# Extra pieces of seven attention steps moved to the groups without values, projections in pieces of 512 columns

## The reference

```python
xn = layernorm(x)
# attention: 16 heads of 8 channels
q, k, v = heads(xn @ Wq.T), heads(xn @ Wk.T), heads(xn @ Wv.T)
q = q * cos + rotate_half_interleaved(q) * sin     # k alike
attn = softmax(q @ k.T * 8 ** -0.5) @ v
# mixture of 8 experts, the two best of each row
gates = softmax(xn @ gate_w + gate_b); top 2 of 8
h = gelu(xn @ w1[e] + b1[e]); h = gelu(h @ w2[e] + b2[e])
ffn = sum over the two of gate * (h @ w3[e] + b3[e])
out = x + attn + ffn
```

## Time and profile before

| what | us |
|---|---|
| median of 3 runs | 631.75 |
| span of the profiled execution | 630.1 |
| PE busy | 597.7 (95%) |
| ACT busy | 536.9 (85%) |
| DVE busy | 338.4 (54%) |
| POOL busy | 195.7 (31%) |
| steps 2 to 8, from the first exponential of step 2 to the last of step 8 | 86.84 to 299.84 |

### The profile page before, as it was taken

How to read it: one execution, slowest core, us unless ns; L and a number is a source line. 1 busy time by engine, 2 the same in 40 slices (tenths; PEclk the granted TensorE clock), 3 DMA queues, 4 the chain that set the end, 5 groups by cost and what they waited for, 6 DMA issues and landing times.

```text
span 630.1 us, 12248 instructions
## 1 busy us (share of the span) xinstructions
PE 597.7 (95%) x4152; PEld 259.9 (41%) x4152; DVE 338.4 (54%) x819; ACT 536.9 (85%) x548; POOL 195.7 (31%) x187
## 2 busy tenths in 40 slices
PE   9889999999999999998999999999999999999996
PEld 6323333232322222222799999993222222222221
DVE  5654233785343335121555555555494958668475
ACT  3799999999999999999554555559999999999995
POOL 2700000000554444441121222223645648484000
PEclk9999999999999999999999999999999999999999
DMA  8653711523363446693433333310312122121311
GB/s 230 172 196 136 264 36 35 217 101 119 127 218 124 146 147 211 211 302 67 105 81 71 79 75 75 75 44 22 104 36 87 48 69 63 58 84 57 113 44 35
DMA packets 82621, 70.67 MB, mean 112 GB/s; under 512 B 44288, under 2 KB 58400, under 8 KB 82576
## 3 DMA queue, kind: packets, MB, share of 16 engines
q1 hardware_dynamic: 76000, 56.34, 29.5%
q0 software_dynamic: 5856, 13.05, 6.8%
q10 hardware_dynamic: 720, 0.71, 0.5%
HBM read 32.92 MB, written 32.96 MB: 105 GB/s over the span
## 4 chain that ended last, share of the span: by engine, by line
PE 64%; ACT 16%; issue 10%; DVE 5%; DMA 2%; ACTq 0%; SPq 0%; DVEq 0%
PE ps L1496 13%; PE ps L1430 10%; ACT probs L731 9%; PE ps L1480 8%; PE ps L1553 6%; PE ps L1422 5%; PE ps L1443 5%; ACT probs L696 4%; PE ps L1526 4%; PE ps L1403 4%; PE ps L1347 2%; ACT probs L674 2%; DMA k_st<-k_d 2%; PE ps L1383 2%; PE ps L1310 1%
## 5 line engine op out<-in xcount | busy, mean ns | idle before, releaser
L696 ACT ACTIVATE probs<-ps 128x1536 f32<-128x1536 f32 (+1 forms) x154 | 206.1, 1426 | 6.7 <-PE ps L1480 6.3
L731 ACT ACTIVATE probs<-ps 128x1536 f32<-128x1536 f32 x140 | 190.2, 1520 | 2.0 <-PE ps L1526 1.9
L574 POOL DMA_INDIRECT slots_x_d<-xn_all,slot_i x64 | 62.5, 977 | 195.7 <-DVE expert_i L1037 127.2
L1496 PE MATMUL ps<-probs,v_st 128*32 128x512 f32 x896 | 119.5, 604 | 1.3 <-DVE v_st L839 0.7
L710 ACT ACTIVATE work<-ps,work 128x256 f32<-128x256 f32 (+1 forms) x156 | 64.9, 454 | 60.5 <-PE ps L1430 60.2
L1553 PE MATMUL ps<-probs,v_st 128*32 128x512 f32 x840 | 111.5, 604 | 0.5 <-DVE o_sb L922 0.5
L612 POOL DMA_INDIRECT work<-slots_y_d,slot_i x64 | 89.8, 1404 | 64.6 <-PE ps L1553 48.4
L1480 PE MATMUL ps<-q_st,k_st 32*128 32x512 f32 x448 | 77.2, 494 | 6.8 <-ACT probs L696 3.7
L1526 PE MATMUL ps<-q_st,k_st 32*128 32x512 f32 x420 | 71.1, 494 | 8.8 <-ACT probs L731 8.7
L1480 PEld LDWEIGHTS ps<-q_st,k_st 32*128 32x128 f32 x448 | 28.9, 181 | 114.6 <-ACT probs L696 80.0
L1526 PEld LDWEIGHTS ps<-q_st,k_st 32*128 32x128 f32 x420 | 26.4, 181 | 108.0 <-ACT probs L731 99.0
(11 more groups left out here) (193 smaller groups left out, 564.3 us busy)
## 6 DMA issues: line engine op xcount, KB each, us to landing
k_d<-parts SPq DMA_DIRECT2D x8, 1024.0 KB, 5.3
q_d<-parts SPq DMA_DIRECT2D x8, 1024.0 KB, 6.1
q_st<-q_d SPq DMA_DIRECT2D x30, 256.0 KB, 3.3
k_st<-k_d SPq DMA_DIRECT2D x30, 256.0 KB, 3.2
slots_x_d<-parts SPq DMA_DIRECT2D x5, 1024.0 KB, 7.5
work<-slots_x_d SPq DMA_DIRECT2D x128, 32.0 KB, 1.9
slots_y_d<-work POOLq DMA_DIRECT2D x32, 128.0 KB, 2.2
work<-work SPq DMA_DIRECT2D x24, 128.0 KB, 2.1
```

The source lines that it names most:

```text
L696: nc.scalar.activation(group_probs(phase, g)[:, 0:size, :], group_slot(g)[:, 0:size * HALF].rearrange("p (h n) -> p h n", n=HALF), ACT.Exp ...
L731: nc.scalar.activation(late_probs(g), group_slot(g).rearrange("p (h n) -> p h n", n=HALF), ACT.Exp, scale=SCALE).then_inc(S["exp_done"], 1)
L1496: ins = nc.tensor.matmul(o_ps[32 * h:32 * h + 32, :], v_window(mt, h, half), group_probs(phase, half * HALF_GROUPS + g)[:, n, :], start=(j ...
```

## The change

All extra pieces of steps 2 to 8 stand at the six places whose groups have no values (blocks' places 0, 4, 6, 8, 12 and 14, iterations g = 1, 5, 9, 12, 16, 20). The projections of batches 1 to 3 are twelve pieces of 512 columns, one to a part, and VectorE reads each with two operations on 512 columns. The joins get new blocks: parts 4 to 15 were joined at blocks 42, 46, 50, 57, 70, 76, 82, 90, 100, 108, 114, 118. The last values piece goes from place 2 to 6 of step 2, norm 1 from the end of step 3 to the start of step 4, the bound from place 2 to 0 of step 8, the first four routing pieces from blocks 35, 40, 41, 43 to 39, 42, 43, 44, and the routing's exponential from before group 7 to before group 11.

```diff
-JOB_PLACE = {1: 0, 3: 2, 5: 4, 7: 5, 9: 6, 12: 8, 14: 10, 16: 12, 18: 13, 20: 14}
+JOB_PLACE = {1: 0, 5: 4, 9: 6, 12: 8, 16: 12, 20: 14}
...
-    fixed = {0: ("values", 0, 2), 7: ("norm", 0), 62: ("norm", 1), 94: ("norm", 2), 126: ("norm", 3), 54: ("count",),
-             BLOCKS * 8 + 2: ("bound",)}
+    fixed = {0: ("values", 0, 2), 7: ("norm", 0), 64: ("norm", 1), 94: ("norm", 2), 126: ("norm", 3), 54: ("count",),
+             BLOCKS * 8: ("bound",)}
...
-    for g, places in enumerate(((37, 38, 42), (40, 42, 46), (45, 46, 50), (50, 53, 57),
-                                (64, 66, 70), (70, 72, 76), (74, 78, 82), (80, 86, 90),
-                                (88, 96, 100), (102, 104, 108), (106, 110, 114), (112, 114, 118)), 4):
-        for part in range(2):
-            fixed[places[part]] = ("plain", g, part)
-        joins[places[2]] = g
+    for g, (made, joined) in enumerate(((40, 43), (44, 48), (46, 50), (56, 60), (70, 74), (76, 80), (78, 82), (86, 90),
+                                        (92, 96), (102, 106), (108, 112), (112, 116)), 4):
+        fixed[made] = ("plain", g)
+        joins[joined] = g
...
-ROUTE_EXP = (2, 7)
-ROUTE = {divmod(block, BLOCKS): n for n, block in enumerate((35, 40, 41, 43, 47, 49, 51, 52, 53, 54, 55, 56, 57, 58, 59, 60, 61, 62, 63, 65, 66))}
+ROUTE_EXP = (2, 11)
+ROUTE = {divmod(block, BLOCKS): n for n, block in enumerate((39, 42, 43, 44, 47, 49, 51, 52, 53, 54, 55, 56, 57, 58, 59, 60, 61, 62, 63, 65, 66))}
...
-                sp.wait_ge(S["aux_read"], AUX[("plain", g, 1)] + 1)
+                sp.wait_ge(S["aux_read"], AUX[("plain", g)] + 1)
...
-                nc.vector.tensor_tensor(t_cos[:, u, lo:lo + HALF // 2], aux_ps[:, 0:HALF // 2], cos_sb[:, cols], ALU.mult)
+                nc.vector.tensor_tensor(t_cos[:, u, :], aux_ps, cos_sb[:, cols], ALU.mult)
...
-                nc.vector.scalar_tensor_tensor(rot[:, u, lo:lo + HALF // 2], aux_ps[:, 0:HALF // 2], -1.0, sin_sb[:, cols],
-                                               ALU.mult, ALU.mult).then_inc(S["aux_read"], 1)
+                nc.vector.scalar_tensor_tensor(rot[:, u, :], aux_ps, -1.0, sin_sb[:, cols], ALU.mult, ALU.mult).then_inc(S["aux_read"], 1)
...
-                nc.tensor.matmul(aux_ps[:, 0:HALF // 2], weights(g, 0), xnT[:, b, lo:lo + HALF // 2],
-                                 start=True, stop=True).then_inc(S["aux_done"], 1)
+                nc.tensor.matmul(aux_ps, weights(g, 0), xnT[:, b, lo:lo + HALF], start=True, stop=True).then_inc(S["aux_done"], 1)
```

More of the change, by code:

```diff
@@ L459, in _ @@
                     job = JOBS.get((t, j), ("none",))
-                    if job[0] == "plain" and job[2]:
+                    if job[0] == "plain":
                         exchange_rows(job[1])
@@ L886, in copy_values, with plain_part @@
                 gate_logits(b, n, aux_ps).then_inc(S["aux_read"], 1)
-            def plain_part(g, part):
+            def plain_part(g):
                 u, m = g % 2, g // 2 % 2
-                lo = part * (HALF // 2)
-                cols = slice(m * HALF + lo, m * HALF + lo + HALF // 2)
-                dve.wait_ge(S["aux_done"], AUX[("plain", g, part)] + 1)
+                cols = slice(m * HALF, (m + 1) * HALF)
+                dve.wait_ge(S["aux_done"], AUX[("plain", g)] + 1)
                 dve.wait_ge(rot_made[u], g // 2)
                 dve.wait_ge(hi_made[u], g // 2)
-                nc.vector.tensor_tensor(t_cos[:, u, lo:lo + HALF // 2], aux_ps[:, 0:HALF // 2], cos_sb[:, cols], ALU.mult)
+                nc.vector.tensor_tensor(t_cos[:, u, :], aux_ps, cos_sb[:, cols], ALU.mult)
                 dve.wait_ge(lo_made[u], g // 2)
@@ L1116, in _ @@
                     elif job[0] == "plain":
-                        plain_part(job[1], job[2])
+                        plain_part(job[1])
                     elif job[0] == "norm":
@@ L1341, in turn_batch_rows, with project @@
                 ins.then_inc(S["aux_done"], 1)
-            def project(g, part):
-                b, lo = g // 4, g // 2 % 2 * HALF + part * (HALF // 2)
-                free_aux(AUX[("plain", g, part)])
-                nc.tensor.matmul(aux_ps[:, 0:HALF // 2], weights(g, 0), xnT[:, b, lo:lo + HALF // 2],
-                                 start=True, stop=True).then_inc(S["aux_done"], 1)
+            def project(g):
+                b, lo = g // 4, g // 2 % 2 * HALF
+                free_aux(AUX[("plain", g)])
+                nc.tensor.matmul(aux_ps, weights(g, 0), xnT[:, b, lo:lo + HALF], start=True, stop=True).then_inc(S["aux_done"], 1)
             def count_tokens():
@@ L1456, in extra_piece @@
                 elif job[0] == "plain":
-                    project(job[1], job[2])
+                    project(job[1])
                 elif job[0] == "norm":
```

## The result

The changed kernel takes 628.42 us (median of 6 runs, 627.79 to 628.8), the kernel before in the same sessions 632.24. The ratio is 0.9931, with a 95% interval of 0.992 to 0.9942, so the change makes it 0.7% faster, by 3.8 us in the medians.

A forecast was written before the change was run, and what follows sets the result against it. ScalarE looked like the bound, with TensorE's 1.43 us groups holding it back unseen. Terms -9.2 + 4.2 + 0.4 + 0.1 + 0.7 were given as -3.7, from 631.75 to 628.1 us, range 626.5 to 631.3.

The forecast's parts named there:

- 1.43 us is TensorE's rhythm: Steps 2 to 8: a group with values takes TensorE 1.43 us, a little more than ScalarE's 1.33 to 1.35.
- The rival by which only open gaps count: Steps 2 to 8: only ScalarE's idle 6.7 us can go, about half stays or returns; 629.9 us, 8%.
- Placing and keys, -9.2 with 2.3 of it keys: Steps 2 to 8, pieces at narrow cost, nothing late: -9.2 us; 2.3 key waits, 0.8 late copy, 6.1 parts.
- The width, +4.2: Twelve wide projections, each holding TensorE 1.06 us for a narrow one's 0.63: +4.2 us on the path.
- both bounds (0.87 and 1.26): Wide projection's TensorE time in us: 0.87 with the 0.20 hidden gives -5.9; 1.26, two narrow ones, gives -1.5.
- the 0.20 us beside the stream: TensorE time of a narrow projection beyond its 0.43 us of streaming, assumed the same for a wide one.
- Routing, +0.4: Step 2, routing's exponential before group 11: VectorE's maximum ready 0.5 us too late, +0.4 us.
- The count, +0.1: Step 3: the count's masks come from VectorE at 13.2 us into the step with 12.7 wanted, +0.1 us.
- Step 4's keys, +0.7: Step 4: keys wait for part 7's late store, land 7.1 us into the step with 6.1 wanted, +0.7 us.
- the slower rival: Steps 3, 4 and 5: keys landing late; at 8.2 us into their step 1.8 us slower, 633.5; 7%.
- The forecast by steps: Steps 2 to 8 were put at 31.2, 29.7, 30.9, 29.7, 29.3, 29.2 and 29.0 us.
- no gap of ScalarE behind a part: Expected in the profile after: ScalarE shows no gap behind any part; no size given.

The follow-up runs named there:

- experiment 2: Changed kernel with the seven turns one iteration later, beside values (iteration 6 in place of 5): 631.27 us, 0.9983 of before.
- experiment 6: Kernel before, 256-column pieces; the sixteen of steps 4 to 7 put in groups without values, no store ahead of keys: 629.31 us, 0.9938 of before.
- experiment 3: Kernel before with the stores of parts 9 and 13 one block later, behind the keys of steps 5 and 7: 629.72 us, 0.9949 of before.
- experiment 5: Changed kernel with the routing's exponential before group 13 of step 2 in place of group 11: 628.04 us, 0.992 of before.
- experiment 4: Changed kernel with part 7 joined one block earlier, at 59: 628.11 us, 0.9921 of before.
- experiment 1: Changed kernel with each wide piece made as two products of 256 columns back to back: 628.38 us, 0.9927 of before.

## Why the prediction was right, point by point

*Which engine sets the pace.* The reading that 1.43 us is TensorE's rhythm and 1.33 ScalarE's own holds: experiment 2 brings gaps back by place alone, and steps 4 and 6 of experiment 6 take 29.2, which is TensorE's own sum. But most of what was won was in plain sight: 2.6 of the 3.4 us are ScalarE's idle time, and 0.8 the rhythm that no idle column shows. The rival by which only open gaps count had the gain too small (629.9) because it let half of the 6.7 us stay or come back, and 4.1 of them did.

*Placing and keys, -9.2 with 2.3 of it keys.* Experiment 3 measured 2.1 for the keys. Experiment 2 measured 2.3 for seven pieces beside values where 2.7 had been expected. The -9.2 and the +4.2 were not measured apart, only what is left of both: the 3.4 us of the seven steps, with the 0.5 and 0.67 of the two new waits added (experiments 5 and 4), are 4.5 (3.37 + 0.5 + 0.67) where the forecast has 5.0.

*The width, +4.2.* A wide piece was put at 1.06 and takes 1.05, both bounds (0.87 and 1.26) are out. The prediction took the 0.20 us beside the stream over from a narrow projection, which is one product and one piece, and left open which of the two they belong to: it is the piece (experiment 1).

*Routing, +0.4.* The wait was 0.77 us where 0.5 was put; it costs 0.5 (experiment 5). The maximum was taken off 2.3 us behind the start of the values (100.44 to 102.70), for the 2.2 of the sum; the rest is that ScalarE came earlier than summed. *The count, +0.1:* there is no such wait. TensorE starts the count at 131.25, straight behind the scores at 130.82.

*Step 4's keys, +0.7.* The gap is 0.68, and taking it away gives 0.67 (experiment 4). That it fits so well hides two errors that cancel: the store took 4.43 for 4.9, and 0.48 us pass between its landing and the issue of the keys, which the sum had left out. The keys of steps 3 and 5 land 5.1 us into their steps, a little earlier than the 5.2 to 5.6 of the forecast: the slower rival had nothing to stand on.

*Where it was off.* The terms add up to -3.8 and not -3.7. The forecast by steps adds up to 209.0, which is 4.0 below the 213.0 measured before (its rules had started from 212.8), and the seven steps take 209.6: they fell by 3.4. That the medians differ by 3.8, so near to the 3.7, is in part luck. The largest single miss by step is step 8, 29.35 for 29.0. The prediction gives no length for the bound. In the kernel before, values start 0.66 us behind its start, but the last of its eight products runs beside them:

```profile
275.24 0.93 PE L1362 MATMUL ps<-cst,peaks 128*1 128x128 f32 x7
275.90 0.63 PE L1496 MATMUL ps<-probs,v_st 128*32 128x512 f32 x3
...
277.06 0.51 PE L1480 MATMUL ps<-q_st,k_st 32*128 32x512 f32 x3
```

The two together hold TensorE 1.82 us there, 0.82 more than values alone. In the changed kernel scores follow:

```profile
269.78 1.03 PE L1357 MATMUL ps<-cst,peaks 128*1 128x128 f32 x8
270.75 0.51 PE L1475 MATMUL ps<-q_st,k_st 32*128 32x512 f32 x3
```

The bound holds TensorE 0.97 us. Taken at 0.66, it would be 0.31 short, nearly all that step 8 is off; that this is the reason is argued from these rows, no run tried it. And one sentence on the profile after was wrong: "no gap of ScalarE behind a part". Gaps of 0.39 to 0.47 stand at 118.13, 163.73 and 178.75, each where a wide piece comes just ahead of a short group, which lasts 0.9 and not 1.35 on ScalarE, and one of 0.35 at 208.46 behind norm 2, which is about as long as a wide piece (1.0 us). The lengths of steps 3 to 6 came within 0.15 of the forecast all the same. In experiment 6 only the one behind norm 2 is left in steps 4 to 7 (0.36), and none stands behind a narrow piece.

## What to carry to other kernels

Where two engines are both "busy" 96 to 97% of a stretch, compare start to start of one group on each: the few per cent are in the rhythm, and a small piece of work belongs in the iteration in which the engine would wait anyway. If it has to stand elsewhere, leave the free iteration behind it empty. Before making pieces larger, see whether the old size fits into the free places; only where it doesn't can the larger piece be worth its overflow. And read the order of a DMA queue as a critical path: two stores moved behind the loads that the next step waits for were worth more than half of this change.

## What the runs showed of the hardware that was not expected

- A piece of full-width products between those of four heads side by side costs 0.20 us beside its columns, whether one product is in it or two: 1.06 us for four instructions of 256 columns, 1.05 for two of 512 (experiment 1). About half is at its first instruction, half between its end and the next scores.
- A 256 KB load issued 0.6 us behind a 1 MB store on the same queue lands after 5.3 us, and without it after 3.0 to 3.1 (experiment 3).
- Between the landing of part 7's store and the issue of the keys that wait for it on SP, 0.48 us pass (150.93 to 151.41 in the changed kernel, and 0.48 in experiments 1, 2, 4 and 5).
- Eight products with one output row hold TensorE 0.97 us when scores follow. When values follow, these start 0.66 us after the first of the eight, beside the last, and both together take 0.82 more than values alone.
